# Gated cross-attention block: the mask of the transposed scores on TensorE in 32x32 tiles

## What is computed

```python
q = (layernorm(x) @ Wq + bq).reshape(N, 128, 16, 16); k, v from ctx
energy = einsum('nqhd,nkhd->nhqk', q, k)
energy = where(mask == 0, finfo.min, energy)
attn = softmax(energy / sqrt(16), axis=-1)
x = x + tanh(g_xattn) * (einsum('nhqk,nkhd->nqhd', attn, v) @ Wo + bo)
x = x + tanh(g_ffn) * tanh(layernorm(x) @ weight @ aux_weight1 @ aux_weight2 + bias)
```

## Time and profile before

| | before |
|---|---|
| median of three runs | 1119.73 us (1119.67 to 1120.63) |
| profiled execution, first to last instruction | 1118.3 us |
| TensorE busy | 1073.6 us, 96% |
| TensorE, weight loads | 941.8 us, 84% |
| VectorE busy | 966.1 us, 86% |
| ScalarE busy | 826.3 us, 74% |
| GpSimd busy | 774.2 us, 69% |

### The profile page before, as it was taken

The page is one execution under the profiler, slowest core; times in us unless marked ns, Lnnn a source line. Parts: engine busy times, 40 slices in busy tenths (PEclk is TensorE's granted clock), DMA queues, the critical chain, the costliest instruction groups (busy, mean ns, idle before and its releaser), DMA issues.

```text
span 1118.3 us, 45477 instructions
## 1 busy us (share of the span) xinstructions
PE 1073.6 (96%) x18979; PEld 941.8 (84%) x18979; DVE 966.1 (86%) x1272; ACT 826.3 (74%) x1275; POOL 774.2 (69%) x1185
## 2 busy tenths in 40 slices
PE   5989999999999999999999999999999999999975
PEld 4777888888888888888888888888888888888865
DVE  4788888988988988898888898898889889889876
ACT  4465877877887787787777787778778778777842
POOL 5245677777777776776777777777777777777653
PEclk9899999999999999999999999999999999999997
DMA  6134344334434433433433443443443344343232
GB/s 167 30 89 117 77 120 136 102 106 134 110 114 119 128 107 107 135 108 98 136 103 104 136 108 112 123 124 106 112 135 106 102 135 108 113 121 108 71 116 77
DMA packets 160189, 124.78 MB, mean 112 GB/s; under 512 B 91889, under 2 KB 126962, under 8 KB 159986
## 3 DMA queue, kind: packets, MB, share of 16 engines
q1 hardware_dynamic: 159842, 121.61, 38.8%
q10 hardware_dynamic: 144, 0.26, 0.1%
HBM read 69.41 MB, written 51.38 MB: 108 GB/s over the span
## 4 chain that ended last, share of the span: by engine, by line
PE 89%; DVE 5%; issue 2%; SPq 2%; DMA 1%; ACT 0%; DVEq 0%
PE ps_m L455 17%; PE ps_m L448 16%; PE ps_s L573 13%; PE ps_s L546 12%; PE ps_x L585 11%; PE ps_m L510 8%; PE ps_m L442 5%; PE ps_s L552 4%; PE ps_x L563 2%; DVE neg_max L938 2%; DVE probs L949 2%; DMA a_rows<-scratch_a 0%; DMA den<-a_den 0%; SPq L200 0%; PE ps_m L598 0%
## 5 line engine op out<-in xcount | busy, mean ns | idle before, releaser
L949 DVE TENSOR_TENSOR probs<-ps_s,far_T 128x2048 f32<-128x2048 f32 x128 | 293.3, 2292 | 36.8 <-PE ps_s L573 36.6
L938 DVE TENSOR_REDUCE neg_max<-ps_s 128x16 f32<-128x2048 f32 x128 | 291.3, 2276 | 6.4 <-PE ps_s L552 6.3
L748 ACT ACTIVATE probs<-probs 128x2048 f32<-128x2048 f32 x128 | 244.5, 1910 | 7.9 <-DVE probs L949 7.7
L723 ACT ACTIVATE q_aug<-ps_m,q_bias,q_scale 128x256 f32<-128x256 f32 x256 | 123.7, 564 | 161.9 <-PE ps_m L448 152.4
L573 PE MATMUL ps_s<-q_aug,k_aug 32*128 32x128 f32 x4096 | 152.8, 284 | 7.4 <-DVE neg_max L938 3.3
L546 PE MATMUL ps_s<-k_aug,q_aug 32*128 32x128 f32 x4096 | 151.1, 284 | 6.4 <-DVE probs L949 6.1
L573 PEld LDWEIGHTS ps_s<-q_aug,k_aug 32*128 32x128 f32 x4096 | 129.9, 187 | 27.2 <-issue 17.4
L944 DVE TENSOR_TENSOR q_aug<-q_aug,ps_x 128x512 f32<-128x512 f32 x128 | 88.0, 687 | 74.0 <-PE ps_x L563 74.0
L546 PEld LDWEIGHTS ps_s<-k_aug,q_aug 32*128 32x128 f32 x4096 | 126.9, 187 | 28.3 <-issue 28.3
L585 PE MATMUL ps_x<-probs,v_ones 128*32 128x128 f32 x4096 | 139.2, 277 | 3.9 <-issue 2.3
L388 POOL TENSOR_TENSOR y<-y,th 128x512 f32<-128x512 f32 x58 | 74.1, 1278 | 88.7 <-ACT th L769 88.7
(11 more groups left out here) (122 smaller groups left out, 1958.2 us busy)
## 6 DMA issues: line engine op xcount, KB each, us to landing
scratch_a<-a_den SPq DMA_DIRECT2D x64, 512.0 KB, 3.1
x_in<-in_x SPq DMA_DIRECT2D x64, 256.0 KB, 3.7
a_rows<-scratch_a SPq DMA_DIRECT2D x64, 256.0 KB
den_wide<-scratch_r SPq DMA_DIRECT2D x64, 256.0 KB
out<-y SPq DMA_DIRECT2D x64, 256.0 KB, 5.3
ctx_in<-in_ctx SPq DMA_DIRECT2D x252, 64.0 KB, 3.8
den<-a_den SPq DMA_DIRECT2D x128, 8.0 KB
scratch_r<-den_r SPq DMA_DIRECT2D x64, 16.0 KB, 1.4
```

Source lines behind the costliest of these rows:

```text
L723: last = nc.scalar.activation(dst[:, :, 2 * m + a, :], src[:, m * TOK:(m + 1) * TOK].rearrange("p (n q) -> p n q", q=P), ACT.Identity, bia ...
L748: nc.scalar.activation(tile, tile, ACT.Exp).then_inc(probs_ready, 1)
L938: nc.vector.tensor_reduce(out_v, ps_s[:], AX.X, ALU.max, negate=True).then_inc(max_ready, 1)
L949: nc.vector.tensor_tensor(probs[i % 2][:].rearrange("p j s q -> p (j s) q"), ps_s[:].rearrange("p j s q -> p (j s) q"), far_T[:].unsqueeze ...
```

## The change

The mask of the transposed scores is no longer added by VectorE. `scores_T` ends with 16 matmuls of 32x32 tiles (`add_mask(far_T4)`), as `scores` does with `far_4`; both share a function. `far_T` becomes bf16, and SyncE spreads it by 16 DMAs into `far_T4`, in the layout of `far_4`; the first scores_T waits for them. `mask_transposed` and the semaphore `t_masked` are gone: `exponents(i)` waits for `t_done`, reads the score banks and writes `probs`, and `scores` waits for `probs_ready`. Hence exponents(i) also waits for the values product of batch i - 2, which reads the same buffer. In ScalarE's list the exponentials are at other places.

```diff
+            def spread_far_T():
+                sp.wait_ge(farT_ready, 1)
+                for r in range(G):
+                    for c in range(G):
+                        sp.dma_start(far_T4[r * ROWS:(r + 1) * ROWS, c, :], far_T[c * ROWS:(c + 1) * ROWS, :]).then_inc(farT_spread, 16)
...
             load_later()
+            spread_far_T()
...
+            def add_mask(rows_4):
+                for r in range(G):
+                    rows = slice(r * ROWS, (r + 1) * ROWS)
+                    for c in range(G):
+                        last = nc.tensor.matmul(ps_s[c * ROWS:(c + 1) * ROWS, r], ident_4[rows, :],
+                                                rows_4[rows, c, :].unsqueeze(1).to_broadcast([ROWS, SLOTS, P]), start=False, stop=True,
+                                                tile_position=(r * ROWS, c * ROWS), skip_group_check=True)
+                return last
...
-                wait(pe, t_masked, i - 1)
+                wait(pe, probs_ready, i - 1)
...
-                last.then_inc(s_done, 1)
+                add_mask(far_4).then_inc(s_done, 1)
...
+                if i == 0:
+                    pe.wait_ge(farT_spread, 16 * G * G)
                 pe.wait_ge(q_ready2, i + 1)
                 pe.wait_ge(max_ready, min(i + 2, NB))
+                if i == NB - 1:
+                    pe.wait_ge(probs_ready, i)
...
-                last.then_inc(t_done, 1)
+                add_mask(far_T4).then_inc(t_done, 1)
...
             def exponents(i):
-                act.wait_ge(t_masked, i + 1)
-                tile = probs[i % 2][:].rearrange("p j s q -> p (j s q)")
-                nc.scalar.activation(tile, tile, ACT.Exp).then_inc(probs_ready, 1)
+                act.wait_ge(t_done, i + 1)
+                wait(act, pv_done, i - 1)
+                nc.scalar.activation(probs[i % 2][:].rearrange("p j s q -> p (j s q)"), ps_s[:].rearrange("p j s q -> p (j s q)"),
+                                     ACT.Exp).then_inc(probs_ready, 1)
...
-            def mask_transposed(i):
-                dve.wait_ge(t_done, i + 1)
-                wait(dve, pv_done, i - 1)
...
-                if is_batch(2 * t - 1):
-                    mask_transposed(2 * t - 1)
...
-                if is_batch(2 * t):
-                    mask_transposed(2 * t)
```

More of the change, by code:

```diff
@@ L53, in gated_xattn_block @@
         mask_i, mask_4 = sb("mask_i", [P, P], I32), sb("mask_4", [P, G, P], I32)
-        far, far_T = sb("far", [P, P]), sb("far_T", [P, P])
+        far, far_T = sb("far", [P, P]), sb("far_T", [P, P], BF16)
         far_4, ident_4 = sb("far_4", [P, G, P], BF16), sb("ident_4", [P, ROWS], BF16)
+        far_T4 = sb("far_T4", [P, G, P], BF16)
         ident_sum = sb("ident_sum", [P, ROWS])
@@ L128, in gated_xattn_block @@
             "consts_ready", "zeros_ready", "ones_ready", "spreads_ready", "scales_ready", "biases_ready"))
-        w_high, wk_ready, wq_ready, wv_ready, far_ready, far_turned, farT_ready = (sem(n) for n in (
-            "w_high", "wk_ready", "wq_ready", "wv_ready", "far_ready", "far_turned", "farT_ready"))
+        w_high, wk_ready, wq_ready, wv_ready, far_ready, far_turned, farT_ready, farT_spread = (sem(n) for n in (
+            "w_high", "wk_ready", "wq_ready", "wv_ready", "far_ready", "far_turned", "farT_ready", "farT_spread"))
         product_done, product_kept, gates_ready, out_weight, bias_done, bo_ready, out_high, wo_ready, wf_ready, bv_ready = (
@@ L143, in gated_xattn_block @@
         xn_ready, yn_ready = sem("xn_ready"), sem("yn_ready")
-        (s_done, max_ready, max_turned, q_ready2, t_done, t_masked, probs_ready, pv_done, a_ready) = (sem(n) for n in (
-            "s_done", "max_ready", "max_turned", "q_ready2", "t_done", "t_masked", "probs_ready", "pv_done", "a_ready"))
+        (s_done, max_ready, max_turned, q_ready2, t_done, probs_ready, pv_done, a_ready) = (sem(n) for n in (
+            "s_done", "max_ready", "max_turned", "q_ready2", "t_done", "probs_ready", "pv_done", "a_ready"))
         ln_step, ln_v_step, x_step, y_step = sem("ln_step"), sem("ln_v_step"), sem("x_step"), sem("y_step")
@@ L572, in scores_T @@
                         rows = slice(j * ROWS, (j + 1) * ROWS)
-                        last = nc.tensor.matmul(ps_s[:, j, s, :], k_aug[p % 2][rows, n, s, :], q_aug[p % 2][rows, n, s, :],
-                                                start=True, stop=True, tile_position=(j * ROWS, 0))
-                last.then_inc(t_done, 1)
+                        nc.tensor.matmul(ps_s[:, j, s, :], k_aug[p % 2][rows, n, s, :], q_aug[p % 2][rows, n, s, :],
+                                         start=(s == 0), stop=False, tile_position=(j * ROWS, 0), skip_group_check=True)
+                add_mask(far_T4).then_inc(t_done, 1)
             def weigh_values(i):
@@ L793, in _ @@
             for t in range(NP):
-                if is_batch(2 * t - 2):
-                    exponents(2 * t - 2)
                 if is_batch(2 * t - 3):
@@ L800, in _ @@
                     gate(t - 6)
-                if is_pair(t + 1):
+                if t < 4 and is_pair(t + 1):
                     spread_q(t + 1)
@@ L804, in _ @@
                     exponents(2 * t - 1)
+                if t >= 4 and is_pair(t + 1):
+                    spread_q(t + 1)
                 if is_pair(t + 1):
@@ L814, in _ @@
                     high_of_a(t - 3)
+                if is_batch(2 * t):
+                    exponents(2 * t)
                 if is_pair(t + 1):
@@ L827, in _ @@
             y4, y3, y2, y1, last = (NP - n for n in range(5, 0, -1))
-            exponents(NB - 2)
             tanh(END)
@@ L1087, in _ @@
             bias_f(END)
-            mask_transposed(NB - 1)
             divide_last_a(y2)
```

3 lines of the change are left out of this document (removed).

## The result

The changed kernel takes 1203.43 us (median of four runs, 1201.12 to 1205.89) against 1119.7 us before: 1.0747 times as long, with a 95% interval of 1.0723 to 1.0771. The forecast was 1211 us, in a range of 1185 to 1240. The profiled execution's span is 1204.0 us, 85.7 more than before.

The account below looks back on a forecast made before the run. TensorE's own stream was taken as the bound. Per pair 0.72 us for masks plus 0.79 for the wait, 1.51 by 62 pairs = 93.6, less 2, on 1118.3 gives 1209.9; with 1.4 for the median, 1211 us, range 1185 to 1240.

Parts of the forecast that it names:

- The bound: Whole loop: TensorE's own stream, busy 96% of the span, bounds the kernel, with score banks handed round without slack.
- The masks: End of scores_T on TensorE: 16 added 32x32 masks per batch cost 0.36 us, 0.72 per pair.
- The bound of 0.66: Masks of scores_T, going on to full 128x128 matmuls: high end of their price, 0.43 plus 0.23 us.
- The exponentials: ScalarE reading score banks instead of SBUF: 1.88 to 1.90 us, bounded by 1.80 and 2.05; waiting on probs_ready costs nothing.
- The chain through ScalarE and VectorE: From scores_T(2t) through exponentials, copies, low_of_x, stats and maxima to the next scores_T: 8.97 us, against 8.18 for TensorE alone.
- the wait at 0.79: TensorE at scores_T waits 0.79 us for the maxima in the first half of every pair.
- hand-over of 0.03: From xT's copy on ScalarE to low_of_x on VectorE: an estimated 0.03 us.
- The start: SyncE's 16 DMAs at 0.46 us each, issued by 27.1 before the first scores_T at 32.93: costed at nothing.
- the cover: Start: 5.8 us left for the last far_T4 DMA to land; if it fails, once 2 to 4 us.
- The end: Last batch: VectorE's last mask of 2.28 us leaves the path, its substitute is 0.47; 2 us of gain.
- The span before: Base of the forecast: a span of 1118.3 us, to which the 62 pairs' cost was added.
- The sum: Whole kernel: 62 pairs by 1.51 = 93.6, less 2, on 1118.3 gives 1209.9 us; 1211 as median.

Follow-up runs that it names:

- the old order: Changed kernel with ScalarE's list in the order of the kernel before, exponents(2t - 2) at the head of the turn: 1526.74 us.
- the two cures: Two one-move variants of the changed kernel: high_of_x(t + 2) directly behind exponents(2t), 1166.44 us; maxima(2t) ahead of low_of_x(t + 1) and stats_of_x(t + 3, 0), 1174.98 us.

## Why the prediction held, point by point

**The bound.** Right for this change: what was added to TensorE came out in full (45 us for 46), and what was taken from VectorE gave 7 us at most. The prediction took TensorE's stream for the bound all through, with little room to spare. The experiment with the masks of scores taken away shows more exactly that it is so behind scores_T, where the change puts its masks, and that ahead of scores_T VectorE's chain is as long.

**The masks.** Right in size, 0.36 a group. The bound of 0.66 for the way to full tiles was too careful: the step from the masks to L456 or L518 is 0.36 to 0.37. The Trainium skill's rule that a change of tiling mode drains the array (TensorEngine Tiling (Array Packing), Key Properties) adds nothing here beyond that 0.36. Its 660 ns for 16 packed tiles with 512 columns (TensorE: Matmul & The Clock Gate, Part 3) is no price for this loop, where 0.43 us are shown and 0.36 are paid; 0.65 are shown where the clock is 1.2 GHz (728.00 in the old order).

**The exponentials.** 1.883 us from PSUM, inside 1.88 to 1.90. In the steady turns no scores wait for probs_ready; the 8.7 us that TensorE waits on it are those of the start and the end.

**The chain through ScalarE and VectorE.** Right in each link, shown by the two cures. It was forecast at 8.97 us and is 8.91, the wait at 0.79 and is 0.70: the exponentials, the copies and the maxima are each 0.01 to 0.02 shorter than the sum had them. A pair is 17.83 for 17.90. My hand-over of 0.03 from ScalarE to VectorE is shown: xT ends at 578.36 and its remainder begins at 578.39.

**The start.** Mis-sized. I cost the 16 DMAs of far_T4 at 0.46 us of issue each with 5.8 us left over. They took 0.68 on average, 0.59 as a rule and 1.37 once:

```profile
19.78 10.93 SPq L277 DMA_DIRECT2D far_T<-far_T  x16
```

SyncE is free at 30.7, not 27.1, and the last lands just as the first scores_T could start (32.13, against 32.93 before), so the cover held by nothing; the kernel with earlier maxima shows the 5.4 us that were behind it. What the start did cost came from elsewhere: in the first four turns scores wait 1.74, 0.49 and 2.18 us for exponentials behind the copies for q, and behind the two long waits the granted clock is 0.85 and 0.83 over the half (46.25 to 57.76, 84.75 to 94.93), where it was 1.00 before. The start is 11.0 us longer, where 5.5 pairs by 1.51 would be 8.3.

**The end.** I had 2 us of gain from VectorE's last mask, so the last half pair and the end together would have come 1.2 us sooner; they come 0.4 sooner. The gain at its own place is there: the last values product waits 0.47 us where it waited 2.06. The wait of 1.76 us for exponentials in the last turns is no new one, as scores waited 2.14 us for VectorE's mask there.

**The span before.** The middle of the kernel before is 923.4 us, 5.6 more than 56 x 16.39: a few stops of TensorE for no reason that the profile shows. The three largest, 0.79 to 1.18 us, lie inside a group of scores_T:

```profile
521.79 0.50 PE L573 MATMUL ps_s<-q_aug,k_aug 32*128 32x128 f32 x7 [1.18 <-issue]
```

The middle after is 998.5, and 56 x 17.83 is 998.5. I had counted these stops as if they stayed. That they are fewer in this profiled execution is seen, why is not.

**The sum.** The forecast of the span was 1209.9 us and the profiled one is 1204.0, 5.9 less. The middle was forecast 9.5 too high (3.9 for the pair, 5.6 for the stops), the start 2.7 and the end 0.8 too low. So the mechanism and its size are right, and the sum is closer than its parts, since the start and the end were wrong the other way. The median of the runs, 1203.43, lies 7.6 under the 1211, as the profiled execution was the slowest of the four. (The error of 19 us about 1211 that the forecast allowed gives 1192 to 1230, not 1190 to 1232; its range does not rest on that.)

## What to carry to other kernels

A step taken off an engine that is not the bound is worth only the waits for it. What replaces it on the bounding engine costs its full footprint, if no other engine's chain of equal length runs beside it at that place: read the footprint from start to start in the timeline, and look whether the next hand-over waits for another engine anyway. Behind scores_T the 16 masks cost 0.36 us each time, ahead of it they were free. When an engine's step becomes the one that frees a buffer, it must move forward in its list, and then everything it overtakes is late by its length: follow these steps to the next engine's queue, and look what stands behind the waiting instruction there. Here moving one copy or one reduction by a few lines gave back 38 us in the middle, with no instruction changed; of the whole 84 us the copy gave back 37 and the reduction, whose move delays the start, 28.

## What I had not expected of the hardware

With waits of TensorE of 2.2 to 2.7 us twice a pair, the granted clock fell to 1.2 GHz 46 times in the 112 halves of the middle, which adds 1.4 us to a pair. Single waits of 1.74 and 2.18 us in the start of the changed kernel had the same behind them. With waits of 0.7 us once a pair it stayed at 1.00.

A DMA of 8 KB from SBUF to SBUF held SyncE's queue longer than a load from HBM of 256 KB: 0.59 us is the median of the 16 for far_T4, and 0.57 that of the 128 for den (`den<-a_den`, kernel after), where the loads of x took 0.40 us in the median and 0.46 in the row that the forecast went by the earlier trace rows.

And the price of the same 16 matmuls was 45 us added at one place and 12 us removed at another of the same kernel, in its steady loop 0.73 us a pair against 0.03.
